# One graph layer with attention: the gathers of the message sum wait tile by tile and run in the order of the weighing

## The reference

```
h_e = einsum('nf,hfd->hnd', x, W_e)                  # what a node sends
ex = exp(alpha_t - m[src])                           # one weight an edge and head
denom = segment_sum(ex, src, N)[src]
att = ex / (denom + EPS)
msg = att[:, :, None] * transpose(h_e[:, dst])       # a row of 512 numbers an edge
out = segment_sum(msg, src, N)                       # summed by the edge's source node
```

## Time and profile before

| | us |
|---|---|
| median of 3 runs | 1552.4 |
| lowest and highest | 1549.43, 1554.43 |
| the profiled execution | 1539.93 |
| its span, first to last instruction | 1538.2 |
| PE, DVE, POOL, ACT busy in the span | 1298.7, 1103.4, 819.0, 736.6 |
| `sum_messages` from its first matmul to its last | 795.5 to 1231.3 |

### The profile page before, as it was taken

The page is one execution under the profiler, slowest core; times in us unless marked ns, Lnnn a source line. Parts: engine busy times, 40 slices in busy tenths (PEclk is TensorE's granted clock), DMA queues, the critical chain, the costliest instruction groups (busy, mean ns, idle before and its releaser), DMA issues. The chain is left out here.

```text
span 1538.2 us, 24695 instructions
## 1 busy us (share of the span) xinstructions
PE 1298.7 (84%) x6804; PEld 821.6 (53%) x6805; DVE 1103.4 (72%) x2257; ACT 736.6 (48%) x1237; POOL 819.0 (53%) x858
## 2 busy tenths in 40 slices
PE   6999967999999999999857875969695947899985
PEld 2555534555555555555435654747473823677762
DVE  8998867999999999989886653848474787122116
ACT  5555416878888888888810000000000083555542
POOL 2110045666666666666266876767676610456541
PEclk9999968999999999999968976989697966899998
DMA  8233367888888888898477867666666327344478
GB/s 237 83 124 139 120 230 232 277 261 267 284 261 291 270 279 273 268 286 261 126 202 236 278 206 212 208 212 185 192 184 202 104 81 276 103 131 135 133 246 294
DMA packets 141702, 322.65 MB, mean 210 GB/s; under 512 B 30163, under 2 KB 46279, under 8 KB 141595
## 3 DMA queue, kind: packets, MB, share of 16 engines
q0 software_dynamic: 62816, 212.87, 44.6%
q1 hardware_dynamic: 74524, 103.15, 20.4%
q10 hardware_dynamic: 4256, 5.24, 1.0%
HBM read 255.27 MB, written 65.93 MB: 209 GB/s over the span
## 5 line engine op out<-in xcount | busy, mean ns | idle before, releaser
L1292 PE MATMUL m_ps<-msg,hot 128*128 128x260 f32 x1344 | 342.7, 414 | 95.6 <-issue 69.0
L1128 POOL DMA_INDIRECT rows<-he_d,target x234 | 295.7, 1264 | 123.1 <-issue 67.9
L1292 PEld LDWEIGHTS m_ps<-msg,hot 128*128 128x128 f32 x1344 | 266.9, 204 | 171.6 <-issue 131.9
L927 PE MATMUL gs_ps<-room,hot_t 128*128 x1008 | 278.0, 386 | 6.3 <-DVE hot_t L782 3.7
L1003 ACT ACTIVATE rows<-rows,raw_a 128x512 f32<-128x512 f32 x336 | 273.5, 814 | 11.2
L1001 ACT ACTIVATE rows<-d_ps 128x512 f32<-128x512 f32 x336 | 196.2, 584 | 98.5 <-PE d_ps L940 51.1
L793 DVE TENSOR_TENSOR rows<-rows 128x512 f32<-128x512 f32 x336 | 229.4, 683 | 9.2 <-ACT rows L1003 5.0
L1208 DVE TENSOR_TENSOR msg<-rows,room 128x512 f32<-128x512 f32 x336 | 211.7, 684 | 20.1 <-DMA rows<-he_d,target 17.6
L1145 ACT COPY room<-m_ps 128x520 f32<-128x520 f32 x20 | 11.8, 592 | 415.4 <-PE m_ps L1292 280.0
L764 POOL DMA_INDIRECT x_sb<-table_d,target x150 | 150.1, 1000 | 96.9 <-PE d_ps L940 65.8
L789 DVE TENSOR_TENSOR x_sb<-x_sb,gs_ps 128x512 f32<-128x512 f32 x204 | 138.8, 681 | 29.2 <-remote 11.5
(11 more groups left out here) (341 smaller groups left out, 1780.1 us busy)
## 6 DMA issues: line engine op xcount, KB each, us to landing
rows<-early_d SPq DMA_DIRECT2D x84, 256.0 KB
early_d<-x_sb SPq DMA_DIRECT2D x51, 256.0 KB
x_sb<-local_d SPq DMA_DIRECT2D x84, 128.0 KB
early_d<-rows SPq DMA_DIRECT2D x33, 256.0 KB
table_d<-rows POOLq DMA_DIRECT2D x10, 520.0 KB, 3.3
both_d<-rows POOLq DMA_DIRECT2D x10, 520.0 KB, 4.4
he_d<-he SPq DMA_DIRECT2D x20, 256.0 KB, 2.0
both_d<-he SPq DMA_DIRECT2D x20, 256.0 KB, 2.3
```

The lines of the kernel that those rows point to most:

```text
L927: pe.matmul(gs_ps[:, use(n, t) % 3, :], h, hrs[:, bass.ds(blk, 1), piece, :].rearrange("p a f -> p (a f)"), start=(piece == 0), stop=(piec ...
L1128: pool.indirect_dma_start(g[:, r, t, :, :, :].rearrange("p c h d -> p (c h d)"), None, he_d, bass.IndirectOffsetOnAxis(ap=k["target"][:, q ...
L1292: last = pe.matmul(m_ps[:, bass.ds(turn[t] & (SLOTS - 1), 1), j, 0:HEADS // 2 * HW].rearrange("p a f -> p (a f)"), hot[:, r, t, :], halves ...
```

## The change

POOL gathers the three tiles of a group from t = 2 down to 0, the order in which they are weighed, instead of 0 up to 2. Before each gather it waits for that tile's own home. For t = 2 that is after the second multiplication of group n - 6, for t = 1 after the third, and for t = 0 after the fourth, as before.

```diff
             for n in range(AHEAD, G):
                 r, q = n % ROWS, first_tile(n)
-                pool.wait_ge(made, GT * (n - ROWS + 1))
-                for t in range(GT - 1):
+                for t in range(GT - 2, -1, -1):
+                    pool.wait_ge(made, GT * (n - ROWS) + GT - t)
                     pool.indirect_dma_start(g[:, r, t, :, :, :].rearrange("p c h d -> p (c h d)"), None, he_d,
                                             bass.IndirectOffsetOnAxis(ap=k["target"][:, q + t:q + t + 1], axis=0)).then_inc(got[r], 16)
```

## The result

| | before | changed |
|---|---|---|
| median of 4 runs, us | 1550.9 | 1513.8 |
| lowest to highest, us | 1543.6 to 1554.4 | 1509.8 to 1516.3 |
| profiled execution, us | 1539.9 | 1512.2 |
| first gather's start to last gather's end, us | 413.3 | 376.6 |
| gathers over 2.5 us | 27 | 0 |

The ratio is 0.975 with an interval of 0.971 to 0.978, so the change takes off 37 us, 2.5%. I had forecast 22 us, 1.4%: the right way and a time inside my range, but the gain was 1.7 times what I took for the likeliest.

The account below looks back on a forecast made before the run. POOL's gather chain of 413.3 us, in a loop of waits with DVE and PE, was taken as the stage's length. Freed groups, 20.5 us, and 2 us of earlier starts made 22 us less: 1530 us, range 1512 to 1563.

Parts of the forecast that it names:

- Starved gathers as the excess: In POOL's chain, 74.3 us of gathering above the median pace, mostly gathers of 2.80 and 4.27 us held behind DVE's multiplications.
- I take half of the starved groups as freed: In the five long stretches between POOL's restarts, 26 of 52 groups stop starving, at 0.79 us each: 20.5 us.
- rival D: Slower: the new phase after each POOL restart starves, decided at the third gather; 1562 to 1568 us, chance 0.23.
- 0.79 us a group as the price: Cost of starvation in the stage: long stretches between restarts take 5.53 us a group, short ones 4.74.
- A: Main case: half of POOL's starvation goes, 1530 us, own range 1512 to 1540, chance 0.38.
- Earlier starts, 23.6 us: At POOL's restarts: 12.4 us from four missed copies avoided, 11.2 from nine starts 1.24 us earlier; only 2 us counted.
- The order and the further waits at nothing: Gathering 2, 1, 0 and waiting before every gather of a group were each claimed to change nothing by themselves.
- B: POOL's restarts come earlier but starvation stays as before: 8 to 12 us gained, 1542 us, chance 0.21.
- C: No gain: the early gather hangs until the same copy that let it in before; 1552 us, chance 0.16.
- E: POOL holds DVE: each gather at a restart delays a multiplication by up to 0.946 us; 1580 us, chance 0.02.
- POOL's pace makes PE slow: In the stage, long full-pace gathering by POOL slows PE's own issue until POOL fills six places and stops; mechanism unknown.

Follow-up runs that it names:

- gaps on DVE: Kernel before, with DVE waiting before each multiplication for the one before it in all groups, not only the first eight: 1520.0 us, ratio 0.979; at 1387 us level 1.014.
- first gather alone: Changed kernel, but only a group's first gather waits for its own home, the other two for the whole group: 1514.0 us, ratio 0.976; at 1387 us level 0.999.
- 128-column version: Changed kernel with a GpSimd write of 128 columns, and a wait for the previous write, behind each gather: 1487.0 us, ratio 0.959.

## Why the prediction was right and wrong

**Starved gathers as the excess: right.** Both ways of letting a gather in ended it, an earlier start and gaps on DVE.

**"I take half of the starved groups as freed": wrong, and this is the step that failed.** All were: 27 gathers over 2.5 us became none. I had found the evidence for the two steps at hand, a gather that gets in at a border between multiplications, and starvation kept up only by its own phase. Then I hedged on the third gather. My rival D said what decides: it starves if it starts 0.07 us before a border. At 843.04 it starts close to that and takes 0.97 us. The multiplications that begin at the two borders, in the changed kernel behind the gather of 843.04 and in the kernel before behind the starved one of 845.70:

```profile
843.12 0.68 DVE L1208 TENSOR_TENSOR msg<-rows,room 128x512 f32<-128x512 f32 x1
```

```profile
845.78 0.68 DVE L1208 TENSOR_TENSOR msg<-rows,room 128x512 f32<-128x512 f32 x1
```

At 0.01 us both are 0.08 us away; in the traces' nanoseconds it is 83 and 77, and that is the difference. I take all gathers that started 66 to 100 ns before a border between two multiplications, in five traces of the 1550 us level (before, order alone, changed twice, first gather alone). From 66 to 77 ns all 41 were held for over 2 us, from 81 ns on none of 134, and between these 12 of 18, where I don't know what else decides. All of the held ones are from the two kernels with the old wait, and within a run of slow gathers one start sets the next, so they are no independent draws.

The third gather behind a restart of the changed kernel started, where it fell near such a border, 79 to 86 ns before it. So D's sign was nearly right, and its outcome was missed by some nanoseconds. That the start two multiplications earlier fell on the good side was luck of the phase and nothing that my rows to 0.01 us could have told. The restarts of the changed kernel are so alike that the outcome is one for all of them, so a half was the least likely value. In the kernel before they were not: of its 11 waits for DVE, four ended in a gather of 4.27 us and the others didn't.

**0.79 us a group as the price: a little high.** All 52 groups freed would be 41 us, and 2 more for earlier starts, 43 in all; measured were 37. POOL's chain has 78 groups and took 4.83 us a group in the changed kernel, near the 4.74 of the short stretches. With 0.70 us a group 52 groups make 36.6. So the main miss is the fraction, a half where it was all, and the price hid a part of it. My signs for A, 8 to 15 gathers of 2.8 us and a mean of 1.14 us, were missed on the same side: none, and 1.02 us.

**Earlier starts, 23.6 us: mostly no gain of their own.** Restarts became 21 instead of 11, and waiting grew by 22.1 us. The 3.1 us of a missed copy are part of starvation. The gaps on DVE, with no earlier start allowed, brought 33 us at the price of a slower DVE.

**The order and the further waits at nothing: right** (order alone 0.999; first gather alone 0.976).

**Rivals.** B and C expected 20 or more long gathers: none. D expected more than 30. E would show in the multiplications; they take 671 to 734 ns, where it was 673 to 733, so a gather that passes costs DVE no more than before. So a gather of 0.95 us that passes between two multiplications doesn't hold DVE for 0.95 us, and DVE's side of the rule that E rests on isn't seen here. POOL's side is: a gather that starts 0.10 us or more before a border between multiplications ends about 0.90 us behind it, so it was held until the multiplication ended (1.15 us for those 0.25 us ahead). By the rule in the Trainium skill, SBUF — State Buffer, section "Who interferes with whom", both sides would be held; the trace agrees for POOL and not for DVE, and the starved gathers were held over several multiplications.

**POOL's pace makes PE slow: half shown.** It needs the 1550 us level; at 1387 us POOL goes on at full pace and PE is never slow. At 1550 us the order in time fits: in the kernel before no instruction of PE's sequencer is slow from 840 to 870 us, while gathers starve, and the first comes 9 us after POOL is at full pace again (861.2). In the changed kernel the first slow ones come 7 to 9 us after the restarts at 840.34, 858.41 and 873.63. A gather every 1.51 us in place of 1.30 took nearly all slow instructions away, but that edit also moved the gathers against DVE's pattern, so the pace isn't shown alone. The bytes aren't the cause. The mechanism stays open, and so does the question why the levels differ.

## What to carry to other kernels

Where one engine's instruction has to slip in between another's, look at the length of the single instruction, not at the mean: a run of equal long ones, exactly one in each period of the other engine, is a phase that locks, and where the first one starts decides those that follow until a pause. One such run is there wholly or not at all. Where all its starts are alike, so is the sum, and a forecast should carry both ends and no half; and where a few nanoseconds decide, it should say that it can't know which end. A change worth 2.5% on one level of a chip can be worth nothing on another: here the loss was there only where PE's sequencer was slow at times.

## What the runs showed of the hardware

- The same kernel took 1387 us in some comparisons and 1550 in others, each stable within 1%. In the stage, the longest of PE's register instructions (FUSED_REGOPS) takes 165 ns at the first and 1392 ns at the second (changed kernel).
- A gather of POOL (0.95 us) ran beside DVE's multiplications with two inputs in two ways, held 1.85 us once in each 3.10 us or hardly at all, by its phase. With starts 66 to 77 ns before the next multiplication it was the first (41 of 41), with 81 to 100 ns the second (134 of 134).
- A write of 0.14 us on POOL behind a gather costs next to nothing (ratios 1.002 and 1.003 in the kernel before), since it lies in the gap of 0.30 us; one of 0.22 us widens it to 0.38.
- More work on the engine that seemed to bound the stage made the kernel 27 us shorter (1514 to 1487), with 13 slow instructions of PE's sequencer where there were 104. At 1387 us, where nothing is slowed, this 128-column version wasn't measured.
